# Expert down projection: high and low weights side by side in one 512-column matmul, added at eviction

## The reference

```python
xg = flat_x[topk_idx]                      # 16 experts x 1024 tokens x 256
g = jnp.einsum('ecd,eid->eci', xg, Wg)     # inner width 1024
u = jnp.einsum('ecd,eid->eci', xg, Wu)
h = jax.nn.gelu(g, approximate=False) * u
eo = jnp.einsum('eci,edi->ecd', h, Wd)     # the down projection
eo = eo * topk_weight[..., None]
flat_out = jnp.zeros_like(flat_x).at[topk_idx.reshape(-1)].add(eo.reshape(-1, d))
shared = jax.nn.gelu(hidden @ Sg.T, approximate=False) * (hidden @ Su.T) @ Sd.T
x = x + layernorm(flat_out + shared)
```

## Time and profile before

| | us |
|---|---|
| median of 3 runs (lowest to highest) | 2098.47 (2097.11 to 2100.47) |
| the profiled execution | 2097.01 |
| its span, first to last instruction | 2095.2 |
| TensorE busy | 2025.3 (97%) |
| VectorE busy | 1192.6 (57%) |
| ScalarE busy | 968.2 (46%) |
| GpSimd busy | 435.0 (21%) |
| granted TensorE clock, mean | 0.986 |

### The profile page before, as it was taken

One profiled execution on the slowest core, in us unless ns is written; L12 is line 12 of the kernel. 1 busy time (PEld: TensorE's weight loads), 2 busy tenths in 40 slices (PEclk: granted clock), 3 DMA queues, 4 the chain that ended last, 5 costly groups with the idle time before them and its releaser, 6 DMA issues.

```text
span 2095.2 us, 33169 instructions
## 1 busy us (share of the span) xinstructions
PE 2025.3 (97%) x12826; PEld 1810.7 (86%) x12826; DVE 1192.6 (57%) x2527; ACT 968.2 (46%) x1802; POOL 435.0 (21%) x449
## 2 busy tenths in 40 slices
PE   7999999999994999999999999999999999999996
PEld 6899999999993888888888989898988888888885
DVE  5586686686664887564545455535353535444565
ACT  4464564574552344443434343434353434444443
POOL 0000000000001000224222422232223222332265
PEclk9999999999996999999999999999999999999998
DMA  3011110111014211233333323333333333334266
GB/s 114 1 41 42 61 63 41 60 61 52 30 63 178 77 56 56 98 87 64 90 62 82 73 72 79 75 80 77 78 88 66 93 64 89 76 79 101 54 199 130
DMA packets 55622, 159.94 MB, mean 76 GB/s; under 512 B 9536, under 2 KB 26048, under 8 KB 48320
## 3 DMA queue, kind: packets, MB, share of 16 engines
q1 hardware_dynamic: 28976, 116.16, 15.3%
q0 software_dynamic: 26512, 41.96, 12.5%
HBM read 98.78 MB, written 59.31 MB: 75 GB/s over the span
## 4 chain that ended last, share of the span: by engine, by line
PE 64%; DVE 2%; POOL 1%; ACT 0%; DMA 0%; issue 0%; DVEq 0%; SPq 0%; ACTq 0%; POOLq 0%
PE mo_psD L58 7%; PE mo_psD L60 7%; PE mo_psD L59 7%; PE mo_psG L58 7%; PE mo_psU L58 7%; PE mo_psG L60 7%; PE mo_psG L59 7%; PE mo_psU L60 7%; PE mo_psU L59 7%; PE mo_psX L1164 1%; PE mo_psX L980 1%; DMA mo_F<-ACC 0%; DVE mo_st L1456 0%; POOL mo_rs L1748 0%; DVE mo_HF L1492 0%
## 5 line engine op out<-in xcount | busy, mean ns | idle before, releaser
L1492 DVE TENSOR_TENSOR mo_HF<-mo_psU,mo_HF 128x512 f32<-128x512 f32 x320 | 221.2, 691 | 637.7 <-ACT mo_HF L1333 637.6
L1333 ACT ACTIVATE mo_HF<-mo_psG 128x512 f32<-128x512 f32 x320 | 191.5, 599 | 475.5 <-PE mo_psU L60 471.6
L1720 POOL DMA_INDIRECT ACC<-mo_OUT,mo_GI x128 | 202.7, 1584 | 681.0 <-ACT mo_OUT L1400 671.5
L60 PE MATMUL mo_psD<-mo_wd_hi,mo_H_lo 128*128 128x256 f32 x1024 | 289.8, 283 | 0.0
L59 PE MATMUL mo_psD<-mo_wd_lo,mo_H_hi 128*128 128x256 f32 x1024 | 289.8, 283 | 0.0
L58 PE MATMUL mo_psD<-mo_wd_hi,mo_H_hi 128*128 128x256 f32 x1024 | 289.6, 283 | 0.0
L1437 DVE TENSOR_TENSOR mo_H_lo<-mo_HF,mo_H_hi 128x512 fp32r<-128x512 f32 x300 | 204.4, 681 | 0.0
L1311 ACT ACTIVATE mo_H_hi<-mo_HF 128x512 fp32r<-128x512 f32 x320 | 199.4, 623 | 1.0 <-DVE mo_HF L1492 1.0
L59 PEld LDWEIGHTS mo_psD<-mo_wd_lo,mo_H_hi 128*128 128x128 f32 x1024 | 196.5, 192 | 1.2
L58 PEld LDWEIGHTS mo_psD<-mo_wd_hi,mo_H_hi 128*128 128x128 f32 x1024 | 196.5, 192 | 1.2
L60 PEld LDWEIGHTS mo_psD<-mo_wd_hi,mo_H_lo 128*128 128x128 f32 x1024 | 196.5, 192 | 0.0
(11 more groups left out here) (255 smaller groups left out, 5154.3 us busy)
## 6 DMA issues: line engine op xcount, KB each, us to landing
X1a<-wg_in SPq DMA_DIRECT2D x16, 1024.0 KB, 4.9
X1a<-wu_in SPq DMA_DIRECT2D x16, 1024.0 KB, 4.9
X1a<-wd_in SPq DMA_DIRECT2D x16, 1024.0 KB, 4.9
XN<-XNB SPq DMA_DIRECT2D x8, 1088.0 KB, 4.1
X<-x_in SPq DMA_DIRECT2D x8, 1024.0 KB, 6.4
out_dram<-X SPq DMA_DIRECT2D x8, 1024.0 KB, 4.4
XN2T<-xn2T SPq DMA_DIRECT2D x8, 1024.0 KB, 3.8
mo_F<-ACC SPq DMA_DIRECT2D x7, 1024.0 KB, 12.7
```

Source lines behind the costliest of these rows:

```text
L60: return pe.matmul(out, w_lo, x_hi, start=False, stop=last)
L1333: a.activation(HF[:, it % 2, :], psG[:, it % 2, :], ACT.Gelu).then_inc(s_gelu, 1)
L1492: v.tensor_tensor(HF[:, it % 2, :], psU[:, it % 2, :], HF[:, it % 2, :], ALU.mult).then_inc(s_mul, 1)
L1720: g.indirect_dma_start(out=io["ACC"], out_offset=bass.IndirectOffsetOnAxis(ap=GI[n % 2][:, 4 * tb + t:4 * tb + t + 1], axis=0), in_=OUT[:, ...
```

## The change

The wd pair becomes one tile [128, 2, 8, 256] at the same place, with the high weights in its first half and the low ones in its second. In an expert block's down projection the matmuls H_hi x wd_hi and H_hi x wd_lo become one matmul of 512 columns that writes both halves of the PSUM bank: the high product to columns 0 to 255, the low one to columns 256 to 511. H_lo x wd_hi is accumulated to the first half as a second matmul. The eviction is then two steps: ScalarE copies the first half times TW to OUT and counts up a new semaphore `s_half`; VectorE waits for it, computes second half times TW plus OUT in place, and counts up `s_ev`. The list parts in VectorE's `down` are placed between these steps: `v_lo1` ahead of tile 0's, `v_hival` ahead of tile 2's. The shared blocks are as before.

```diff
+    def both(self, n, s):
+        t = self.new(n, [s[0], 2] + s[1:], F32R)
+        self.place[n + "_hi"] = self.place[n]
+        self.place[n + "_lo"] = self.place[n] + 4 * int(np.prod(s[1:]))
+        return t
...
-        wd = pair("wd", [P, NI, D])
+        wd_both = mem.both("wd", [P, NI, D])
+        wd = [wd_both[:, z, :, :] for z in (0, 1)]
...
-                        i = mm3(pe, psD[:, t % 2, 0:D], H[0][:, z, t * P:(t + 1) * P], H[1][:, z, t * P:(t + 1) * P],
-                                wd_hi[:, it, :], wd_lo[:, it, :], it == 0, it == n - 1)
+                        h_hi, h_lo = (x[:, z, t * P:(t + 1) * P] for x in H)
+                        if is_e(b):
+                            pe.matmul(psD[:, t % 2, :].rearrange("p (z d) -> p z d", z=2), h_hi, wd_both[:, :, it, :],
+                                      start=(it == 0), stop=False)
+                            i = pe.matmul(psD[:, t % 2, 0:D], h_lo, wd[0][:, it, :], start=False, stop=(it == n - 1))
+                        else:
+                            i = mm3(pe, psD[:, t % 2, 0:D], h_hi, h_lo, wd_hi[:, it, :], wd_lo[:, it, :], it == 0, it == n - 1)
...
-                        a.activation(OUT[:, t, :], psD[:, t % 2, 0:D], ACT.Copy, scale=scale).then_inc(s_ev, 1)
+                        i = a.activation(OUT[:, t, :], psD[:, t % 2, 0:D], ACT.Copy, scale=scale)
+                        i.then_inc(s_ev if is_b(b) else s_half, 1)
...
-                if 0 <= h < NCH - AHEAD:
-                    topk.v_lo1(v, AHEAD + h)
-                    topk.v_hival(v, AHEAD + h)
+                if is_e(b):
+                    n, tb = expert(b)
+                    for t in range(4):
+                        if h < NCH - AHEAD and t == 0:
+                            topk.v_lo1(v, AHEAD + h)
+                        if h < NCH - AHEAD and t == 2:
+                            topk.v_hival(v, AHEAD + h)
+                        wait(v, s_half, 4 * h + t + 1)
+                        v.scalar_tensor_tensor(OUT[:, t, :], psD[:, t % 2, D:2 * D], TW[n % 2][:, 4 * tb + t:4 * tb + t + 1], OUT[:, t, :],
+                                               ALU.mult, ALU.add).then_inc(s_ev, 1)
```

More of the change, by code:

```diff
@@ L1085, in moe @@
         s_up, s_gelu, s_mul, s_hhi, s_hlo = (sem(n) for n in ("s_up", "s_gelu", "s_mul", "s_hhi", "s_hlo"))
-        s_dn, s_ev = sem("s_dn"), sem("s_ev")
+        s_dn, s_ev, s_half = sem("s_dn"), sem("s_ev"), sem("s_half")
         s_xt, s_xhi, s_xlo = sem("s_xt"), sem("s_xhi"), sem("s_xlo")
@@ L1219, in down @@
                 if is_e(b):
-                    wd_hi, wd_lo = wd
                     if expert(b)[1] == 0:
```

## The result

Twelve executions of each kernel, side by side: 2093.15 us in the median (2089.93 to 2096.52) against 2099.24 (2097.11 to 2102.18). The ratio is 0.9973 with a 95% interval of 0.9964 to 0.9982, so the change is faster by 0.27%, 6 us by the medians. The forecast was 2085.6 (range 2078 to 2093), 13 us under the median of the kernel before that it started from (2098.47). The sign was right, the size was half of it, and the median lies 0.15 us above the range. The profiled execution took 2095.7 us.

The account below looks back on a forecast made before the run. TensorE's matmul stream was taken to bound the expert stage. Cheaper matmuls (-13.4 us) and the last block's hand-over (+0.5) gave -12.9 us, so 2085.6 us from a median of 2098.47, range 2078 to 2093.

Parts of the forecast that it names:

- What bounds, and that no bank comes late: Expert stage: TensorE's matmul stream bounds it; PSUM banks return in time, 1.2 us spare at tile 2.
- Rival D: Expert down projection: VectorE's add hands the PSUM bank back late, eating the gain; times around 2098 us, 2%.
- The eviction's price: Expert blocks' eviction: VectorE's added step takes 479 ns, 128 times, 61 us more on VectorE, hidden in the stage.
- the hand-over: End of the last expert block: ScalarE's copy passes to VectorE's add, 0.48 plus 0.03 us, +0.5 us.
- (2): Expert down projection: alternating 512 and 256 columns bounded by seams, 0.342 to 0.352 us a pair, 0.3466 kept.
- My upper bound: Expert down projection: dear end of a pair's price, 0.352 us, which saves 8 us.
- A: Expert down projection: each 512 behind a 256 pays the seam's dearest gaps; saves 8 to 0 us, 10%.
- Rival C: Expert down projection: the moving operand's break in SBUF restarts the stream; +99 us, about 2198 us, 5%.
- E: Expert down projection: the wide matmul is carried out as two of 256; no gain, 2099 us, 3%.
- Rival B: Expert down projection: each 256 costs the 0.11 seam, 512s stay at 0.2267; saves 20 to 23 us, 10%.

Follow-up runs that it names:

- evict_only: Kernel before with only the new two-step eviction, still three 256-column matmuls (high x low to the bank's second half): 2101.28 us, ratio 1.0011.
- after_c: The changed kernel run again without edits: ratio to the kernel before 0.9965 (0.9951 to 0.9978).
- grouped: Changed kernel with each token tile's eight 512-column matmuls first, then its eight of 256: 2088.57 us, ratio to before 0.9959.
- evict_warm: evict_only plus eight useless matmuls ahead of the third tile's wait behind the experts: 115.15 us from last expert down projection's start to the end.
- probe: Changed kernel, another matmul stream per expert: 0 as changed, 1 with the 512 columns unbroken (both 352.8 ns a pair), 2 three of 256 (119.9 ns each).
- before_a: The kernel before, unedited, profiled again to see the spread between executions: 2101.43 us (one execution).
- before_b: The kernel before, unedited, profiled once more for the same spread: 2099.34 us (one execution).
- no_add: Changed kernel without VectorE's add, so the second half of each bank is left out of the result: 2095.64 us, ratio to before 0.9964.
- grouped_last: grouped with its last expert block made as before (three matmuls of 256, one-step eviction): 2094.37 us, ratio to before 0.9962.

## Why the prediction was right in sign and wrong in size

**What bounds, and that no bank comes late: right.** TensorE is without waits in the stage, and evict_only leaves it at 1077.63 us. In the changed kernel's fullest kind of block (from 976.01) tile 0's add began at 979.79 and took 0.48, and tile 2 began at 981.65: 1.4 us to spare, where I had 1.2. Rival D falls. **The eviction's price: right** at 484 ns and 0.51 us for the hand-over.

**The step that failed is (2), the price of a pair.** It came out at 0.3528 us, not 0.3466: 7.1 us from 1024 groups, not 13.4. I had the right rows and took them for prices of a single seam. The first 256 behind 512s (0.11) and the six 512s behind 256s (0.2317) were the start and the course of a recovery that lasts over several matmuls. In an alternation it never ends, and then the cheap 0.11 isn't paid each time: it comes once in three, and the wide ones reach 0.241. My upper bound, 0.232 + 0.12 = 0.352, was what came to pass; I put the forecast between the bounds because plain means fell there. Of the rivals, A (each wide one pays the seam, the narrow one stays at 0.12) gave 0.352 to 0.36 and 2091 to 2099 us. It was what happened, and it had 10%.

**A term was missing behind the block.** The recovery of the 512s that follow is longer (0.233 over nine): 0.036 us a block, 1.2 us in 32. **And one at the end:** behind the longer stand ahead of the third tile the clock was granted at 0.50, 1.5 us. The sum as the traces have it is -7.1 + 1.2 + 0.5 + 1.5 = -3.9 us, with up to 1.5 us either way from when the accumulated rows come. The measured ratios give -5.7 us (-7.6 to -3.8) and, run again as after_c, -7.3 (-10.3 to -4.6). The sum lies just inside the first interval and 0.7 us outside the second; the first three terms alone, -5.4, lie inside both. The fourth comes from profiled executions, which were slow ones for the changed kernel (2095.7 and 2094.3 us with medians of 2093.15 and 2091.53) and a fast one for the kernel before (2097.01 with 2099.24). Whether the median execution pays it is not shown.

**One execution's span was a poor base.** The stages ahead of the experts, which the change doesn't touch, ended at 902.8 to 906.4 us in fourteen traces, before and after mixed. The trace of before had 902.9, that of after 905.1; their spans differ by 1.3 us where the medians differ by 6. The clock goes with this too. In attention's last 40 us it is granted at 0.50, but in four traces (before, after_c, grouped, evict_warm) it is at 1.00 for some microseconds in between, and just these four end at 902.8 to 903.2; the other ten end at 904.8 to 906.4. Before, then after (columns: us, TensorE busy and count, granted clock, DMA share, GB/s):

```profile
652.80:656.00 3.20, 2.51 (x24) 1.00 0.58 246
...
652.80:656.00 3.20, 2.51 (x12) 0.50 0.45 189
```

Rival C (the stream restarts at the break; it had drawn on a section about PSUM for an operand in SBUF) and E (carried out as two of 256) fall with the probe's first experts. Rival B needed each 256 at 0.113.

## What to carry to other kernels

Merging two matmuls of 256 columns into one of 512 is worth 13 ns where all have one width, but saved only 7 ns where wide and narrow ones alternate; set those of one width behind each other (eight and eight took the surplus from 6.2 to 1.7 ns a pair here). When an alternation isn't in the trace, read the distances behind a seam until they are steady, and take the dear end of the bound. Look at the clock behind the places where TensorE stands: here the first stand left it at 1.00 where it was 1.97 to 2.27 us long (five traces) and let it fall where it was 2.99 to 3.97 (seven); the second, of 2.6 us, let it fall in nine of fourteen. Each fall cost some 1.5 us, and two traces of one kernel can differ by one.

## What was not expected of the hardware

- The distance of matmuls depends on more than the two neighbours: a strict cycle of six (0.236, 0.113, 0.233, 0.117, 0.241, 0.120) in the alternation, and ten 512s behind it until the distance stays at 0.227, against five behind 256s. Which unit keeps this memory, no run shows; equal weights for both matmuls changed nothing.
- 448 columns cost 202.7 ns, 16.0 over their columns, where 320, 384 and 512 cost 13.3 to 13.7.
- Mostly in the first twelve expert blocks two matmuls of the up projection now and then started 0.5 to 1.0 us apart with no engine to wait for: four times in before_a, once in before_b, twice in no_add, in six blocks of grouped_last, never in the first trace of before. With smaller delays in six later blocks these made grouped_last's stage 1071.83 us where grouped had 1066.26, which hides what that experiment was to show. What holds them up, no run shows. TensorE's waits there:

```profile
PE mo_psU L59 <- issue: 1.4, 4, 0.4
PE mo_psU L58 <- issue: 0.9, 2, 0.6
PE mo_psU L60 <- issue: 0.2, 1, 0.2
```
